# Attention sweeps of a graph kernel: a second buffer for the sums, and another order of ScalarE's work

## The reference, cut to what matters

```python
def _gat_conv(x, src, dst, W, a_src, a_dst, bias, concat, n_nodes):
    H, C = a_src.shape
    xw = (x @ W).reshape(n_nodes, H, C)
    al_s = jnp.sum(xw * a_src[None], axis=-1)
    al_d = jnp.sum(xw * a_dst[None], axis=-1)
    e = jax.nn.leaky_relu(al_s[src] + al_d[dst], 0.2)
    e_max = jax.ops.segment_max(e, dst, num_segments=n_nodes)
    ex = jnp.exp(e - e_max[dst])
    denom = jax.ops.segment_sum(ex, dst, num_segments=n_nodes)
    msg = xw[src] * (ex / denom[dst])[..., None]
    out = jax.ops.segment_sum(msg, dst, num_segments=n_nodes)
```

## Time and profile before

| what | us |
|---|---|
| median of three runs | 12618.34 |
| profiled execution, its own time | 12618.56 |
| span of its trace | 12616.8 |
| VectorE busy | 5345.2 (42%) |
| GpSimd busy | 6532.0 (52%) |
| ScalarE busy | 2582.5 (20%) |
| TensorE busy | 3962.2 (31%) |

### The profile page before, as it was taken

One profiled execution on the slowest core, in us unless ns is written; L12 is line 12 of the kernel. 1 busy time (PEld: TensorE's weight loads), 2 busy tenths in 40 slices (PEclk: granted clock), 3 DMA queues, 4 the chain that ended last, 5 costly groups with the idle time before them and its releaser, 6 DMA issues. The chain is left out here.

```text
span 12616.8 us, 82629 instructions
## 1 busy us (share of the span) xinstructions
PE 3962.2 (31%) x19153; PEld 2596.1 (21%) x19153; DVE 5345.2 (42%) x6339; ACT 2582.5 (20%) x3818; POOL 6532.0 (52%) x6784
## 2 busy tenths in 40 slices
PE   2667501896333333344000100010002000015877
PEld 2555401453111111244000100010001000003544
DVE  6222285334555555277455322222223466652111
ACT  0333253232222322111000011100110233320000
POOL 0666576002777777374777477747773655540000
PEclk9555555897555555577555555555555555557899
DMA  6000022666888888200666311121111222225899
GB/s 276 3 3 3 12 91 78 230 269 229 270 265 267 266 265 270 55 0 0 176 188 187 67 38 37 36 20 38 37 37 18 60 80 80 81 70 200 323 384 359
DMA packets 586456, 1693.37 MB, mean 134 GB/s; under 512 B 267163, under 2 KB 321858, under 8 KB 568289
## 3 DMA queue, kind: packets, MB, share of 16 engines
q0 software_dynamic: 292720, 608.23, 18.7%
q1 hardware_dynamic: 229648, 722.30, 15.7%
q10 hardware_dynamic: 63952, 361.30, 7.3%
HBM read 1016.07 MB, written 675.24 MB: 134 GB/s over the span
## 5 line engine op out<-in xcount | busy, mean ns | idle before, releaser
L1991 POOL DMA_INDIRECT ring<-tab_gat,at x2352 | 2235.8, 951 | 1082.5 <-issue 719.7
L706 POOL DMA_INDIRECT ring<-z_stn,at x1568 | 1508.2, 962 | 1406.2 <-POOLq L703 912.0
L2159 PE MATMUL keys<-spot,ones 128*128 128x128 f32 x6 | 2.3, 487 | 3766.2 <-PEq L2158 3766.2
L1503 PE MATMUL pair_acc<-pair_w,pair_cell 32*112 32x384 f32 (+1 forms) x1120 | 780.3, 878 | 1261.3 <-PEq L1500 1261.3
L560 POOL DMA_INDIRECT sorted<-rows,at x784 | 759.3, 968 | 761.8 <-POOLq L558 528.5
L706 POOL DMA_INDIRECT ring<-z_conv,at x784 | 767.4, 979 | 386.7 <-issue 249.9
L1082 POOL DMA_INDIRECT adj<-val_a,at_a x784 | 766.0, 977 | 335.3 <-issue 255.2
L1249 PE MATMUL acc<-tile,parts 128*96 128x448 f16 (+1 forms) x3430 | 729.4, 361 | 257.5 <-DVE parts L1173 139.8
L2159 PEld LDWEIGHTS keys<-spot,ones 128*128 128x128 f32 x6 | 1.5, 311 | 3766.9 <-issue 3766.9
L2085 DVE COPY peak<-peak 128x6 f32<-128x6 f32 x112 | 19.8, 176 | 1672.4 <-DVEq L2084 1672.4
L878 PE MATMUL acc<-tail,hot 128*128 128x49 f32 (+4 forms) x588 | 145.8, 432 | 1797.9 <-PEq L876 1797.9
(11 more groups left out here) (453 smaller groups left out, 10619.7 us busy)
## 6 DMA issues: line engine op xcount, KB each, us to landing
tile<-adj SPq DMA_DIRECT2D x490, 784.0 KB, 21.4
z_stn<-block ACTq DMA_DIRECT2D x245, 800.0 KB, 3.3
z_conv<-pair_block ACTq DMA_DIRECT2D x224, 700.0 KB, 6.2
run_gat<-out_rows SPq DMA_DIRECT2D x56, 1596.0 KB, 5.5
adj<-zero SPq DMA_DIRECT2D x49, 1568.0 KB, 38.6
run_basis<-out_rows SPq DMA_DIRECT2D x28, 1750.0 KB, 5.8
ring<-tab_gat,at POOLq DMA_INDIRECT x2352, 2.4
run_gat<-out_rows SPq DMA_DIRECT2D x56, 672.0 KB, 3.1
```

The lines of the kernel that those rows point to most:

```text
L706: g.indirect_dma_start(out=view(bufs[b], k), out_offset=None, in_=table, in_offset=bass.IndirectOffsetOnAxis(ap=at[n][b][:, k:k + 1], axis ...
L1503: last = pe.matmul(self.acc[g][0:self.nodes, n, 0:(hi - lo) * self.fo], self.cell[:, :], cols, start=True, stop=True)
L1991: g.indirect_dma_start(out=ring[b][:, k, :], out_offset=None, in_=tab_gat, in_offset=bass.IndirectOffsetOnAxis(ap=at[b][:, k:k + 1], axis= ...
```

## The change

`sums` becomes two buffers, `sums[b]`, and `sums_ready` and `sums_taken` become one semaphore for each buffer. VectorE sets both `sums_taken{b}` before the loop, waits for the one of its buffer in each chunk, and for both at the end. ScalarE's `chunk` is cut into three functions: `head` (exponentials and decay), `rows` (row copies of a chunk) and `refill` (wait for `ring_free`, stage the next indices). In the loop ScalarE now does `head` of a chunk, then `rows` of the chunk before, then `refill`; the first chunk and the last three are written outside the loop.

```diff
-                sums = sb(st, "sums", [P, NH, per_head, ch])
+                sums = [sb(st, f"sums{b}", [P, NH, per_head, ch]) for b in range(2)]
...
-                    def chunk(b, ahead):
+                    def head(b):
                         a.wait_ge(sem("exps_wanted"), 1)
                         a.sem_inc(sem("exps_wanted"), -1)
                         a.activation(ex, arg[:, 1, :, :], ACT.Exp)
...
+                    def rows(b):
+                        a.wait_ge(sem(f"sums_ready{b}"), 1)
+                        a.sem_inc(sem(f"sums_ready{b}"), -1)
+                        a.wait_ge(sem(f"out_free{b}"), 1)
+                        a.sem_inc(sem(f"out_free{b}"), -1)
+                        a.copy(out_rows[b][:, :, 0:n_sums], sums[b][:, :, :, :].rearrange("p h f j -> p j (h f)"))
+                        a.copy(out_rows[b][:, :, n_sums:n_sums + NH], peak[b][:, :, 1:ch + 1].rearrange("p h j -> p j h")).then_inc(act_step, 1)
+                        a.wait_ge(act_step, 1)
+                        a.sem_inc(act_step, -1)
+                        a.sem_inc(sem(f"chunk_done{b}"), 1)
+                        a.sem_inc(sem(f"sums_taken{b}"), 1)
+
+                    def refill(b, ahead):
                         a.wait_ge(sem(f"ring_free{b}"), 1)
                         a.sem_inc(sem(f"ring_free{b}"), -1)
                         if ahead is not None:
                             stage(b, ahead)
...
-                    with a.Fori(0, steps - 1) as it:
-                        for b in range(2):
-                            chunk(b, it * (2 * ch) + (2 + b) * ch)
-                    for b in range(2):
-                        chunk(b, None)
+                    head(0)
+                    refill(0, 2 * ch)
+                    with a.Fori(0, steps - 2) as it:
+                        for b in (1, 0):
+                            head(b)
+                            rows(1 - b)
+                            refill(b, it * (2 * ch) + (4 - b) * ch)
+                    head(1)
+                    rows(0)
+                    refill(1, (2 * steps - 1) * ch)
+                    head(0)
+                    rows(1)
+                    refill(0, None)
+                    head(1)
+                    rows(0)
+                    refill(1, None)
+                    rows(1)
...
-                            v.wait_ge(sem("sums_taken"), 1)
-                            v.sem_inc(sem("sums_taken"), -1)
+                            v.wait_ge(sem(f"sums_taken{b}"), 1)
+                            v.sem_inc(sem(f"sums_taken{b}"), -1)
...
-                            v.sem_inc(sem("sums_ready"), 1)
-                            v.tensor_copy(carry, sums[:, :, :, ch - 1]).then_inc(dve_step, 1)
+                            v.sem_inc(sem(f"sums_ready{b}"), 1)
+                            v.tensor_copy(carry, sums[b][:, :, :, ch - 1]).then_inc(dve_step, 1)
```

More of the change, by code:

```diff
@@ L2072, in _ @@
                     v.sem_inc(dve_step, -1)
-                    v.sem_inc(sem("sums_taken"), 1)
+                    for b in range(2):
+                        v.sem_inc(sem(f"sums_taken{b}"), 1)
                     carry = tail[:, 0:n_sums].rearrange("p (h f) -> p h f", h=NH)
@@ L2107, in _ @@
                             v.sem_inc(sem("exps_ready"), -1)
-                            v.tensor_tensor(sums[:, :, 1:per_head, :], val_of(ring[b]),
+                            v.tensor_tensor(sums[b][:, :, 1:per_head, :], val_of(ring[b]),
                                             ex.unsqueeze(2).to_broadcast([P, NH, width, ch]), ALU.mult)
                             v.tensor_tensor(fix[:, :, :], carry, first[:, :].unsqueeze(2).to_broadcast([P, NH, per_head]), ALU.mult)
-                            v.tensor_copy(sums[:, :, 0, :], ex).then_inc(dve_step, 1)
+                            v.tensor_copy(sums[b][:, :, 0, :], ex).then_inc(dve_step, 1)
                             v.wait_ge(dve_step, 1)
@@ L2114, in _ @@
                             v.sem_inc(sem(f"ring_free{b}"), 1)
-                            v.tensor_tensor(sums[:, :, :, 0], sums[:, :, :, 0], fix[:, :, :], ALU.add).then_inc(dve_step, 1)
+                            v.tensor_tensor(sums[b][:, :, :, 0], sums[b][:, :, :, 0], fix[:, :, :], ALU.add).then_inc(dve_step, 1)
                             v.wait_ge(dve_step, 1)
@@ L2119, in _ @@
                             v.sem_inc(sem("decay_ready"), -1)
-                            flat = sums[:, :, :, :].rearrange("p h f j -> p (h f j)")
+                            flat = sums[b][:, :, :, :].rearrange("p h f j -> p (h f j)")
                             v.tensor_tensor_scan(flat, decay[:, :, :, :].rearrange("p h f j -> p (h f j)"), flat, 0.0,
```

## The result

The changed kernel takes 12331.69 us (median of four runs, 12303.87 to 12344.5) against 12618.54 us for the kernel before: ratio 0.9771, 95% interval 0.9753 to 0.9789, so 287 us or 2.3% faster. The forecast was 12342 us, the range 12315 to 12400.

The account below looks back on a forecast made before the run. The prediction took convolution 3's sweep to be bound by VectorE, then ScalarE's row copy, in series. Shorter gaps gain 277 us, all other terms 0: 12618.56 - 277 = 12342 us, range 12315 to 12400.

Parts of the forecast that it names:

- The bound: Convolution 3's sweep: bound by the serial chain VectorE, then ScalarE's row copy, at 24.08 us a chunk.
- The gap between chunks: VectorE between chunks of convolution 3: 5.83 us falls to 0.65 inside a turn and 0.95 across; gain 277 us.
- VectorE's own part of a chunk: Convolution 3, VectorE from L2085 to the end of L2126: 18.23 us, giving a chunk of 19.0 us with the gap.
- T: The start of a chunk on VectorE in convolution 3's sweep, from which the prediction timed the other engines.
- The spare time: GpSimd's gathers land before the chunk two ahead starts: 5.2 us to spare at the usual landing, 1.7 at the worst.
- The sweep's end: After convolution 3's last chunk: rows ready at T + 23.7 as before; cost 0, bound 1 us.
- Convolutions 1 and 2: Their sweeps: the wait removed was hidden behind the gathers; gain 0, bounds 1 us either way for each sweep.
- Rival 1: VectorE's product and scan beside ScalarE's row copy slow each other: VectorE stretched by a third, 105 us back, 12446; chance 0.07.
- Rival 2: GpSimd becomes the bound, held by VectorE's short instructions: 21.1 us a chunk, 12455 us; chance 0.05.
- Rival 3: Slower than before: all 14 gathers stretched to 1.74 us, 24.4 us a chunk, 12635 us; chance 0.02.
- Rival 4: No gain: the wait put down to L2084, the sums' buffer, was another's; 12618 us; chance 0.03.
- the 5.83 us: VectorE's wait for the sums' buffer at convolution 3's 55 chunk boundaries, which the prediction said would go.

## Why the prediction was right

*The bound.* The prediction said that one sweep of three is bound by VectorE and ScalarE in series, and that all of the gain would be there: 273 us of it are, and with convolution 3 left out nothing remains.

*The gap between chunks.* Taken at 0.65 us inside a turn and 0.95 across; measured 0.48 and 0.96. The spline sweep's rows were the better guide inside a turn, the first chunk's across one. This alone would have made the gain 281 us.

*VectorE's own part of a chunk.* Taken unchanged at 18.23 us (18.25 in the mean of the sweep before); 19.11 less a mean gap of 0.72 leaves 18.39. That is the other side of it: the product is 0.06 us longer, the wait ahead of the addition of `fix` 0.05 (16.5 us over the sweep against 13.4), and the short instructions together 0.03. The middle one does not come from the overlap that the change made, since the old code in the kernel with the change in convolutions 1 and 2 alone has it too. The two misses have opposite signs, and that is luck: with the gap alone right, the forecast would have been 281 and not 277, against 273.

*ScalarE.* Row copies were to end at T + 12.6; they end at 9867.95, T + 12.7. Staging starts at T + 13.1; the prediction's T + 12.8 was its end, and the 0.44 us of handshake ahead of it (L2018) were left out. ScalarE then waits 9.2 us a chunk for the next exponentials, where about 9 were forecast. Hidden.

*GpSimd.* Its wait for indices was to be 1.3 to 1.6 us a chunk and is 85.0/53 = 1.6. The spare time was reckoned 0.3 us too small (38.0 - 32.5 is 5.5 and not 5.2, 38.0 - 36.0 is 2.0 and not 1.7), unless 0.3 us of start-up were meant, which the prediction does not say; nothing hangs on it.

*The sweep's end.* From the last start to the end it is 24.1 us before and after, so the peeled code and the late store cost nothing there.

*Convolutions 1 and 2.* 970.6 us against 970.2: nothing, as said. The prediction did not see that ScalarE's table load, which the old loop repeated 13 times in convolution 1 (1.28 us each), would now run once; it was off the path, and the sweep's length shows that.

*The rivals.* Rival 1 is real at a thirtieth of its price: 0.06 us a chunk on the product, nothing on the scan. Rival 2 is real too, at hundredths: the largest gather took 1.26 us where it had been 0.98, and the mean went from 943 to 949 ns, 0.08 us for 14 gathers. The prediction's evidence against it was weaker than it looked. In the sweep before, GpSimd stood idle while VectorE added `fix` (L2115, both inputs in SBUF): of 56 additions one had a gather beside it. In the changed kernel 55 have (L2132), and all 11 gathers above 1.1 us lie beside one, started 0.05 to 0.10 us behind it; a gather that had started 0.06 us ahead of it took 0.94. One such pair:

```profile
9884.97 0.54 DVE L2132 TENSOR_TENSOR sums<-sums,fix 128x222 f32<-128x222 f32 x1 [0.34 <-DVEq L2130]
9885.05 1.23 POOL L1991 DMA_INDIRECT ring<-tab_gat,at  x1 [0.30 <-issue]
```

The Trainium skill's rule of the locked port pair (SBUF — State Buffer, Who interferes with whom) has a VectorE instruction with two SBUF inputs contend with a GpSimd instruction that reads SBUF. These pairs agree with it in kind; but held for the whole length of every short instruction, as in rival 2, it would have added 3.7 us to GpSimd's 17.4 a chunk, and the measurement decides for 0.08. Rival 3 would need gathers of 1.42 us in the mean. Rival 4 fell with the 5.83 us.

*The time.* 12342 was forecast from an execution of 12618.56; 12331.69 and 12321.63 were measured in two sets. Beside their own kernels before (12618.54 and 12598.97) they are 287 and 277 us shorter, where the sweep gives 273. What lies beyond the sweep, up to 41 us in the profiled pair, was followed in part only, and there it went with the granted clock. So the test of the model is the sweep, in which the forecast erred by 4 us.

## What to carry to other kernels

When two engines alternate on one buffer, count two loops before adding the second one: that of the buffer, and that of the engine which serves both chunks in its program order. Here the buffer alone gave 169 of 273 us, because ScalarE still did the old chunk's tail before the new chunk's head. And price an instruction to be removed by the distance between its neighbours with and without it, not by its length plus the idle time printed ahead of it: that idle time belongs to the one before.

## What the runs showed of the hardware

- ScalarE's strided copy and VectorE's product from SBUF and PSUM, side by side, are each a little longer than apart: copy 5.57 instead of 5.50 us, product 5.67 instead of 5.61; the same copy beside a scan took 5.52 us and the scan 6.63, as alone.
- An indirect gather of GpSimd that starts just behind a VectorE addition of 0.54 us with both inputs in SBUF took 1.20 to 1.26 us instead of 0.94 (11 gathers of 769); beside the 6.63 us scan with one input in PSUM it stayed at 0.94.
- A loop turn shows in the pitch: VectorE's starts are 18.9 us apart inside a turn and 19.3 across one.
- The same 98 small matmuls with their transposes took 17 us at a granted clock of 0.95 and 29 us at 0.50, in two executions whose code is the same there.
